# Attention with a softmax summed by GpSimd, DMA and TensorE: accumulating transfers re-spaced, and the sum passes one pair of tiles later

## The reference

```python
xn = layernorm(x)
q, k, v = heads(xn @ q_w.T + q_b) / sqrt(32), heads(xn @ k_w.T + k_b), heads(xn @ v_w.T + v_b)
attn = softmax(einsum('bhqd,bhkd->bhqk', q, k))
out = merge(einsum('bhqk,bhkd->bhqd', attn, v)) @ out_w.T + out_b
y = tanh(xn @ weight @ aux_weight1 @ aux_weight2 + bias)
return x + out + y
```

## Time and profile before

| | |
|---|---|
| median of 3 runs | 4234.54 us (4233.6 to 4237.1) |
| the profiled execution | 4234.31 us, span 4232.5 us |
| mean granted TensorE clock | 0.989 of full speed |
| PE busy | 4144.6 us (98%) |
| POOL busy | 3189.9 us (75%) |
| DVE busy | 2932.1 us (69%) |
| ACT busy | 2359.9 us (56%) |

### The profile page before, as it was taken

One profiled execution on the slowest core, in us unless ns is written; L12 is line 12 of the kernel. 1 busy time (PEld: TensorE's weight loads), 2 busy tenths in 40 slices (PEclk: granted clock), 3 DMA queues, 4 the chain that ended last, 5 costly groups with the idle time before them and its releaser, 6 DMA issues.

```text
span 4232.5 us, 77485 instructions
## 1 busy us (share of the span) xinstructions
PE 4144.6 (98%) x21728; PEld 2528.2 (60%) x21728; DVE 2932.1 (69%) x4928; ACT 2359.9 (56%) x4517; POOL 3189.9 (75%) x1119
## 2 busy tenths in 40 slices
PE   7999999999999999999999999999999999999999
PEld 5888888655555555555555555555555555555467
DVE  4344334488877777888877888887788888787334
ACT  2222122156666666666666666666666666666621
POOL 0322232269999999999999999999999999999820
PEclk9999999889999999999999999999999999999999
DMA  4444445447777677777777777777777777777677
GB/s 157 149 165 165 156 145 169 152 96 153 161 152 159 148 156 153 158 159 158 157 153 156 156 156 161 154 155 153 159 153 154 162 160 158 151 156 151 151 242 253
DMA packets 268271, 673.36 MB, mean 159 GB/s; under 512 B 109056, under 2 KB 110080, under 8 KB 214656
## 3 DMA queue, kind: packets, MB, share of 16 engines
q0 software_dynamic: 46080, 335.56, 41.3%
q1 hardware_dynamic: 138784, 220.26, 15.8%
q10 hardware_dynamic: 83040, 113.01, 9.5%
HBM read 195.30 MB, written 137.36 MB: 79 GB/s over the span
## 4 chain that ended last, share of the span: by engine, by line
PE 55%; DMA 9%; issue 7%; POOL 6%; ACT 3%; DVE 1%; POOLq 0%; ACTq 0%; SPq 0%; DVEq 0%
PE pv_bank L860 17%; PE sm_bank L838 16%; PE st_bank L854 16%; POOL pool_sum L642 5%; DMA dma_sum<-probs 5%; DMA q_stack<-max_row 3%; ACT probs L696 3%; PE sm_bank L200 2%; PE sm_bank L860 2%; DVE part_max L774 1%; PE st_bank L200 1%; DMA q_stack<-s_ctx 0%; PE sm_bank L847 0%; POOL dma_sum L653 0%; DVE max_row L758 0%
## 5 line engine op out<-in xcount | busy, mean ns | idle before, releaser
L774 DVE TENSOR_REDUCE part_max<-sm_bank 128x1 f32<-128x512 f32 x4096 | 2498.6, 679 | 576.1 <-PE sm_bank L838 576.0
L642 POOL TENSOR_TENSOR pool_sum<-pool_sum,probs 128x2048 f32<-128x2048 f32 x512 | 2461.4, 4807 | 21.8 <-ACT probs L696 6.3
L696 ACT ACTIVATE probs<-st_bank 128x512 f32<-128x512 f32 x3840 | 1958.3, 614 | 602.1 <-PE st_bank L854 560.7
L838 PE MATMUL sm_bank<-k_stack,q_stack 96*128 96x512 f32 x4096 | 1687.5, 416 | 11.4 <-DVEq L752 9.4
L854 PE MATMUL st_bank<-q_stack,k_stack 97*128 97x512 f32 x4096 | 1647.7, 403 | 37.8 <-DMA q_stack<-max_row 19.3
L838 PEld LDWEIGHTS sm_bank<-k_stack,q_stack 96*128 96x128 f32 x4096 | 785.0, 192 | 543.4 <-DVE part_max L774 331.0
L854 PEld LDWEIGHTS st_bank<-q_stack,k_stack 97*128 97x128 f32 x4096 | 777.3, 190 | 321.9 <-ACT probs L696 141.5
L860 PE MATMUL pv_bank<-probs,v_pair 128*32 128x512 f32 x7680 | 935.4, 602 | 0.0
L860 PEld LDWEIGHTS pv_bank<-probs,v_pair 128*32 128x32 f32 x7680 | 204.7, 109 | 455.5 <-ACT probs L696 259.1
L653 POOL DMA_DIRECT2D dma_sum<-probs x320 | 300.3, 938 | 149.9 <-DMA dma_sum<-probs 141.2
L312 POOL TENSOR_TENSOR y_out<-y_out,x_in 128x512 f32<-128x512 f32 x64 | 82.7, 1292 | 370.7 <-ACT y_out L341 364.7
(11 more groups left out here) (88 smaller groups left out, 2328.7 us busy)
## 6 DMA issues: line engine op xcount, KB each, us to landing
dma_sum<-probs POOLq DMA_DIRECT2D x320, 1024.0 KB, 8.6
q_stack<-s_q_hi ACTq DMA_DIRECT2D x122, 256.0 KB, 6.2
k_stack<-s_k_hi ACTq DMA_DIRECT2D x122, 256.0 KB, 5.0
x_in<-in_x SPq DMA_DIRECT2D x16, 1024.0 KB, 7.8
s_q_hi<-qk_hi SPq DMA_DIRECT2D x16, 1024.0 KB, 4.3
s_q_lo<-qk_lo SPq DMA_DIRECT2D x16, 1024.0 KB, 6.4
s_k_hi<-qk_hi SPq DMA_DIRECT2D x16, 1024.0 KB, 4.3
s_k_lo<-qk_lo SPq DMA_DIRECT2D x16, 1024.0 KB, 6.4
```

Source lines behind the costliest of these rows:

```text
L642: nc.gpsimd.tensor_tensor(total[:], one[:], tile_at(r, kt)[:], ALU.add).then_inc(pool_added, 1)
L696: nc.scalar.activation(tile_at(r, kt)[:, q * BLK:(q + 1) * BLK], st_bank[:, st_place(kt * QB + q)], ACT.Exp, scale=SCALE).then_inc(probs_r ...
L774: nc.vector.tensor_reduce(part_max[:, k:k + 1], sm_bank[:, sm_place(k)], AX.X, ALU.max).then_inc(max_scores_read, 1)
L838: nc.tensor.matmul(sm_bank[:, sm_place(k)], q_st[r][0:ROWS, q * P:(q + 1) * P], k_st[r][0:ROWS, b * BLK:(b + 1) * BLK], start=True, stop=T ...
```

## The change

`JOIN_FIRST` issues a head's first accumulating transfer (tile 2) ahead of GpSimd's first add. The other four (tiles 5, 8, 10, 13) are issued after adds 1, 3, 5 and 7, where they were issued after adds 2, 4, 6 and 7. Each now waits for its own tile's exponentials, since it is issued ahead of the add that implied them. `CUT` goes from 6 to 8, so `add_up` follows the pair that begins with tile 6, and the slot of the sum bank moves from unit 40 to unit 48. DVE's reciprocal comes after unit 60 of the maxima, not 56. ACT copies the sums after tile 7, not 5. The loads are issued after tiles 8, 9, 10, 11, 12, 13 and 15. `heads` can hand a body the following head's index a second time, worked out from i + 2 where the first comes from i + 1 (the number is the same); PE's body takes it as `to_turn` for the maxima.

```diff
-SUM_UNIT = 40
-RECIP_UNIT = 56
-CUT = 6
-LOAD_AT = [6, 7, 9, 10, 12, 13, 15]
+SUM_UNIT = 48
+RECIP_UNIT = 60
+CUT = 8
+LOAD_AT = [8, 9, 10, 11, 12, 13, 15]
-JOIN_AFTER = {0: (0, 1), 2: (0, 2), 4: (0, 3), 6: (0, 4), 7: (0, 5)}
+JOIN_FIRST = (0, 1)
+JOIN_AFTER = {1: (0, 2), 3: (0, 3), 5: (0, 4), 7: (0, 5)}
-        def heads(eng, body):
+        def heads(eng, body, extra=0):
-                after = eng.snap(i + 1)
+                after = [eng.snap(i + 1 + n) for n in range(1 + extra)]
                 for r in range(GROUP):
-                    body(i * GROUP + r, r, GROUP, after * GROUP + (r + 1 - GROUP))
+                    body(i * GROUP + r, r, GROUP, *(a * GROUP + (r + 1 - GROUP - n * GROUP) for n, a in enumerate(after)))
             for r in range(GROUP):
-                body(ALL_HEADS - GROUP + r, r, GROUP - 1 - r, ALL_HEADS - GROUP + r + 1)
+                body(ALL_HEADS - GROUP + r, r, GROUP - 1 - r, *[ALL_HEADS - GROUP + r + 1] * (1 + extra))
             def join(h, r, c, j):
+                pool.wait_ge(probs_ready, PRIME + h * UNITS + QB * (CHAINS[c][j] + 1))
             def sum_up(h, r, i):
+                if i == 0:
+                    join(h, r, *JOIN_FIRST)
                 add(h, r, i)
-            def body(h, r, more, following):
+            def body(h, r, more, following, to_turn):
                 r1 = (r + 1) % GROUP
                 for p in range(CUT // 2, KT // 2):
-                    both_scores(h, r, 2 * p, following, more)
-                    both_scores(h, r, 2 * p + 1, following, more)
+                    both_scores(h, r, 2 * p, to_turn, more)
+                    both_scores(h, r, 2 * p + 1, to_turn, more)
                     use(h, r, 2 * p - 2)
                     use(h, r, 2 * p - 1)
                 if more >= 1:
                     for p in range(CUT // 2):
-                        both_scores(following, r1, 2 * p, following + 1, more - 1)
-                        both_scores(following, r1, 2 * p + 1, following + 1, more - 1)
+                        both_scores(following, r1, 2 * p, to_turn + 1, more - 1)
+                        both_scores(following, r1, 2 * p + 1, to_turn + 1, more - 1)
-            heads(pe, body)
+            heads(pe, body, extra=1)
```

## The result

The changed kernel takes 4531.34 us (median of 4 runs, 4524.65 to 4541.62) against 4235.82 us for the kernel before on the same chip: ratio 1.0699 (95% interval 1.0678 to 1.0721), 296 us or 7% slower. The forecast was 4405 us with a range from 4220 to 4520: direction and place were right, the size was 126 us short, and the time lies 11 us above the range. The profiled execution took 4541.62 us, span 4539.8 us, mean granted clock 0.954.

What follows compares the result with a forecast made beforehand. PE was taken to set the pace, mostly waiting for transfers, with little room on GpSimd beside it. 60 heads x (3.4 - 0.55) = +171 us on the profiled 4234.31 gave 4405 us, range 4220 to 4520.

Steps and rivals of the forecast that it cites:

- the price of a stall, s: PE's stall at a head's first scores, waiting for max_row; forecast 3.4 us per head, ends 2.4 and 5.4.
- The sum: Whole-kernel total: 60 heads x (3.4 - 0.55) = +171 us on 4234.31, giving 4405 us.
- the 0.55 that went before: PE's loss per head before the change, against its own clean cycle: 0.55 us, 35 us in all.
- 48.78: PE's clean cycle in us, from one head's turn to the next, against 49.33 per head on average.
- The meetings of small and large transfers: On DMA, a small transfer issued about 0.9 us or more after a large one lands 0.2 to 1 us after it.
- J3: GpSimd's third of a head's five accumulating transfers; forecast to take 10.0 us and catch the ratio store.
- SP's queue: max_row stands behind four ratio rows, issued in 1.8 us, so leaves 2.4 us after the turn, not 0.6.
- J4 1.1 after the turn, 8.0 to land: Fourth accumulating transfer, issued 1.1 us after PE's once-per-head turn (L847), lands 8.0 later, with max_row 0.5 behind.
- x - s = 19.2, J1 waiting for J5: First accumulating transfer, at x after the turn, waits for the previous head's fifth; x less the stall holds at 19.2 us.
- the way out: Escape at x - s past 19.7, 0.5 us away: ratio store precedes the third transfer, no stall; 4215 us, chance 0.22.
- the milder rival: Last ratio row escapes, scale not late, fourth transfer 1.5 before the turn, stall 1.8 us; 4309 us, chance 0.20.
- Costs at nothing: PE's later sum passes 0, ACT's packed loads 0 (-5 to +10 us), added tile waits free, GpSimd's cycle 49.2 us.

Runs made afterwards that it cites:

- experiment 6: Changed kernel with 10 useless matmuls before the max_row wait: 4524.75 us; Experiment 1's kernel with max_row copied four times: 4518.08 us, with 14 useless matmuls added: 4497.55 us.
- Experiment 1: Changed kernel with each accumulating transfer moving only 512 of 2048 columns (256 KB, not 1 MB): 4192.02 us, ratio 0.9907.
- Experiment 3: max_row issued ahead of the four ratio rows on SP: changed kernel 4300.54 us; changed kernel with the old transfer spacing 4267.34 us.
- experiment 5: Turn of the maxima one tile earlier (unit 4, not 8): kernel before 4244.25 us; changed kernel 4518.68 us.
- experiment 7: Kernel before with ACT's loads packed after tiles 6 to 12, v first: 4220.59 us, ratio 0.9957.
- Experiment 2: Each half alone: kernel before with only the transfers re-spaced, 4262.43 us; changed kernel with the old transfer spacing, 4513.68 us.
- the first filler: Changed kernel with 10 useless matmuls of 512 columns on PE before its wait for max_row: 4524.75 us, ratio 1.0694.

## Why the prediction was right, and where it was wrong

**The step that failed: the price of a stall, s.** "The sum" charged 60 heads with 3.4 us less the 0.55 that went before. PE stands idle 3.16 us per head and needs 0.3 to get going, 3.46 together, so the average wait was sized rightly (by luck in part, see below). But s left out what the stall does to PE's clock. The 62 cycles after the first average 54.37 us, where they averaged 49.37 before; less 48.78, the idle time and the 0.3, 2.13 us per head are left, and all of it lies in heads with time at 1.2 GHz. That is 132 us. The stalls are 62 x (3.46 - 0.59) = 178 us where the sum had 171. The forecast 4405 with 132 and 7 added is 4544, against 4541.62 of the profiled execution. Shown by the two cycles with equal stalls (50.71 and 52.23), and by experiment 6, in which an artificial stall costs the same; filling it halves or better the time at the lower level.

**The meetings of small and large transfers: right.** A small one issued behind J3 or J4 lands with it, 0.2 to 1.8 us later, but for the 17 rows that land with the load of v; the forecast had no such meeting. The Trainium skill, page DMA: Bandwidth & Descriptors, section Queues, rings and completion order, says both that each DMA engine takes its queues in turn, a packet at a time, and that a semaphore's increment lands only after every earlier write of that engine. Experiment 1 agrees with the second, since the row's landing falls from 6.3 to 2.1 us when the large transfer's falls from 8.4 to 3.6; it doesn't tell it from a small transfer that simply stands behind the large one's data.

**SP's queue: right, and larger than said.** I took 1.8 us for the four ratio rows and put the row at 2.4 after the turn. It is 3.64, since one issue takes 1.07 us by the median. A large transfer nearby is not enough for that: before the change the row left 3 to 5 us behind J3 in 30 heads, and its issue took 0.54 all the same. Experiments 3 and 5 show that this order of SP's queue is worth 231 of the 296 us, and that an earlier turn doesn't help.

**J4 1.1 after the turn, 8.0 to land: two errors that cancel.** J4 stands 0.5 us before the next turn on average and takes 8.8. It lands at 8.3 and not 9.1. The row lands 0.6 us after it by the median and 1.1 on average, because of the 17 heads with v's load, where I had taken 0.5: at 9.3 and not 9.6. That the average stall came out near 3.4 is luck in this measure. The forecast had one steady stall; the real ones run from 0.9 to 6.8 us. Of the signs named, the row's median landing, "7 or more", missed too: it is 6.3, because the row leaves later.

**"x - s = 19.2, J1 waiting for J5": wrong.** J1 waits for J5 3 times (8.9 us) and for PE's pass over tile 0 50 times (224.3 us, 52.0 of them once). s is larger than I took it, by the clock's part, and PE is later than J5. In the head shown J1 stands 23.6 after its turn; PE was 4.2 late at the first scores and lost nearly 2 more to the clock, which leaves 17 to 18 for x - s. The margin against the way out was therefore some 2 us and not 0.5 in this head, so that the state holds more firmly than I thought. It is the condition of the milder rival, with the scale late all the same: the scale waits in 60 heads. That rival's J4, 1.5 before the turn and 9 to land, was nearer to what came than mine.

**Costs at nothing: right.** The sum passes, the loads of q and k and the five added waits cost PE nothing in the other seven pairs. The load of v, which stands after tile 15 in both kernels, isn't free here: 17 rows land some 2.2 us later by it than behind J4 alone, 37 us in all. GpSimd's cycle of 49.2 us wasn't put to the test, since PE was the slower of the two. That GpSimd's chain does hold the turns once PE doesn't wait is argued, for the kernel before alone (experiment 5, 49.43 us; experiment 7, 49.03).

**The cause in the change.** The account made it depend on both halves: the store meeting J3, and J4 close to the turn. Experiment 2 shows that the later sum passes, with their reciprocal and loads, suffice: they carry the ratio rows to the turn, and the row behind them. J4 needn't have been moved: it stands 1.6 after the turn there too. But without the even spacing this way costs some 200 us, and 80 more are lost by VectorE's wait for the sums. Experiment 3 shows how much of either goes through the row's place in SP's queue: with the row first, 28 us of the 282 are left, and 65 of the 296 in the changed kernel.

**Open.** Why a DMA issue on SP stretches, and why PE stalls where its loop starts over once the useless matmuls are in it. That an idle PE delays its own J4 and so feeds the next stall is argued from the places of J1 and J4 and the small return of the first filler, not isolated.

## What to carry to other kernels

Before a step on an in-order queue is moved, look at what stands behind it on that queue: here an 8 KB transfer that PE waits for stood behind four that PE does not wait for, and putting it ahead took back 231 of 296 us. Give the latency-critical small transfer a place ahead of bulk issues and away from the start of large transfers. And price a stall of TensorE that comes back in every cycle with the clock it loses: here stalls of 1.6 to 6.8 us cost 0.3 to 5 us more than their length.

## What the runs showed of the hardware that was not expected

- In 52 of the 59 heads with a stall of 1.6 us or more the granted clock fell to 0.5 (1.2 GHz) for 3.4, 6.8 or 10.2 us, during the stall or up to 2 us after work had begun again. Stalls of nearly one length went either way: 1.63 us without a fall, 1.62 with, and 2.04 without.
- One DMA issue of a ratio row took SP 1.07 us by the median where it took 0.42 before, and the row's 1.20 against 0.54.
- An 8 KB transfer landed with whichever large one stood beside it: with J4 in 43 of 61 heads, with the load of v in 17.
- The accumulating transfer of 1 MB took 6.9 us at its shortest and 8.4 by the median, that of 256 KB 3.3 and 3.6: a quarter of the bytes takes nearly half the time.
- With useless matmuls in the wait, PE stalled in every fourth head where its loop over four heads starts over, 1.3 to 2.5 us with fourteen of them and 0.4 to 1.3 with ten, with no releaser in the trace.
